# A two-layer graph network kernel: where sums, counts and normalizations are computed in layer 0

## Chip, cores and metric

One core of one Trainium2 chip. The metric is the device time of one execution in microseconds (us). The engines are TensorE (PE; its weight loads are shown as PEld), VectorE (DVE), ScalarE (ACT), GpSimd (POOL) and SyncE (SP), which issues most of the transfers.

## What is computed

A residual network of two message-passing layers over 6,250 nodes of 128 features and 206,250 edges, sorted by destination. Cut to what matters:

```python
h = relu(layernorm(x))
summed = segment_sum(h[src], dst); counts = segment_sum(ones, dst)
agg = summed / max(counts, 1)
x = x + log_softmax(agg @ W_l.T + h @ W_r.T + b)        # layer 0
h = relu(layernorm(x))
weight = relu(edge_attr @ W1 + b1) @ W2 + b2
x = x + segment_sum((h @ Wl + bl)[dst] * weight, src)   # layer 1
```

The layernorm subtracts the mean of a node's 128 features and divides by the square root of their variance plus 1e-5.

## The kernel before, in words

Nodes lie in 49 blocks of 128 rows (partitions are nodes of a block). For the normalizations seven blocks make a chunk, so there are seven chunks of 128 x 896 elements. Each engine has one program in order, and semaphores tie the programs together; nothing is scheduled at run time, so the order written in the source is the order of each queue.

**Normalization (both layers).** `norm_mean` (L643) on VectorE sums each row of a chunk (L644), scales the sums to means (L645) and subtracts the means from the chunk (L646). `squares` (L1313) on ScalarE squares the result (L1317). `norm_var` (L722) on VectorE sums the squares (L724) and scales them (L725). `deviations` (L1319) on ScalarE takes the square root (L1321). `norm_relu` (L727) on VectorE takes the reciprocal (L729) and scales the positive part (L730). A `link` is a wait of VectorE for its own last instruction. In layer 0, `h0_cut` (L738, VectorE), `h0_high` (L1326, ScalarE) and `h0_low` (L520, GpSimd) then split each value into a high part and a low part, which lie in `h0p`, per block 128 high columns, 128 low columns and two columns of ones. The loop at L741 interleaves these steps: in pass c it takes the mean of one chunk, finishes the chunk of two passes before and sums the squares of the chunk of one pass before. ScalarE's loop at L1329 does, per pass, `squares` of this chunk, `deviations` of the chunk before, `h0_high` of the chunk three passes back.

**Layer 0.** 37 steps of two blocks each, 74 blocks in all, walk over the edges. Per block VectorE makes eight pairs of one-hot tables (`one_hots`, L769), four pairs of buffers deep; PE multiplies them to counts of edges (`step_counts`, L1111), ScalarE copies the counts out (L1360) and, in 32 of the steps, compares node numbers with thresholds (L1352). PE multiplies the finished counts of the block before by `h0p` (`dense`, L1120, 258 columns wide), so that 256 columns hold high and low sums and the last two hold the number of edges per destination. After that, `block_sums` (L774) on VectorE, which stands behind the second pair of one-hots of the next block, waits for the last of the dense products, then adds high and low sums (L777), copies the count (L778), makes a one-hot matrix that places rows at their nodes (L779), and makes a second one scaled by the counts in bf16 (L781). `place` (L1124) on PE, behind the fourth counting step of the block, multiplies the sums by the first matrix in fp32 (L1127) and a matrix of ones by the second in bf16 (L1128). `add_block` (L786) on VectorE, behind the sixth pair of one-hots, adds the two results into the aggregate (L789).

**Between the layers** the loop at L924 (and those at L1388 on ScalarE and L1203 on PE) runs logits, exponentials, logarithms, the second normalization and the product with `Wl`, chunk by chunk, in one interleaved order. **Layer 1** (L1023, L1287, L1462 and the stream of messages, L605) takes the rest of the time.

## Time and profile before

| | |
|---|---|
| median of 3 runs | 3699.18 us (3697.62 to 3706.08) |
| the profiled execution, its own time | 3703.27 us |
| its span in the trace | 3701.4 us |
| PE, VectorE, ScalarE, GpSimd busy | 3077.9, 2796.2, 2089.7, 2207.1 us |
| mean granted TensorE clock, share of full | 0.93 |

The stretches of the span: preparation to about 80 us, the first normalization being its second half; layer 0 to about 910 us; the stage between the layers to 1037 us; layer 1 to the end. In a view of instructions, a number in brackets is the idle time of the engine just before, with the work that ended it. Instructions of one engine overlap at their ends in the trace, so what one of them costs its queue is the distance from its start to the next one's start.

### The profile page before, as it was taken

To read this page: it belongs to the slowest core of one execution; us is meant where nothing else is said; L and a number is where in the kernel's file an instruction comes from. 1 tells how busy PE (TensorE), PEld (TensorE's weight loads), DVE (VectorE), ACT (ScalarE), POOL (GpSimd) and SP (SyncE) were. 2 spreads that over 40 slices of the span, in tenths; PEclk is the share of its full clock that TensorE was granted. 3 is DMA by queue.
4 is the path that set the end of the run, shared out by engine and by line. 5 is a ranking of instruction groups with operands and counts; after the bars stand their busy time and mean duration, and the time that the engine had idled before them with its cause. 6 is when DMAs were issued, how large, how long until landed. Compare 5 with 4: busy or idle time off the path is not lost.

```text
span 3701.4 us, 97235 instructions
## 1 busy us (share of the span) xinstructions
PE 3077.9 (83%) x26330; PEld 2498.3 (67%) x26331; DVE 2796.2 (76%) x7718; ACT 2089.7 (56%) x4907; POOL 2207.1 (60%) x1790
## 2 busy tenths in 40 slices
PE   1799999998677779888888888898888888888867
PEld 0699999997555557666666666666667766666656
DVE  8899999998855557886676766767677777877756
ACT  2699999994532235554454544554455545545546
POOL 4300101000357777777878787878878777878860
PEclk9999999998777779998998989999899999999989
DMA  3298998801034446766776666665677667767757
GB/s 110 70 337 315 319 319 316 316 7 36 12 70 88 88 104 162 175 157 145 151 154 152 135 145 145 154 154 132 144 166 173 161 147 172 172 141 165 174 118 207
DMA packets 576963, 592.90 MB, mean 160 GB/s; under 512 B 71050, under 2 KB 557954, under 8 KB 576689
## 3 DMA queue, kind: packets, MB, share of 16 engines
q1 hardware_dynamic: 449506, 470.49, 44.1%
q0 software_dynamic: 127184, 119.07, 18.2%
q8 instruction: 134, 2.20, 0.2%
q14 instruction: 139, 1.14, 0.1%
HBM read 293.94 MB, written 295.35 MB: 159 GB/s over the span
## 4 chain that ended last, share of the span: by engine, by line
PE 27%; DVE 26%; issue 18%; DMA 12%; POOL 11%; DVEq 5%; ACT 2%; SPq 0%; POOLq 0%; ACTq 0%
DMA messages<-big,idxr 11%; POOL messages L605 10%; PE PS L1120 10%; DVE X L1018 5%; PE PS L1111 5%; PE PS L1283 4%; DVE big L991 3%; DVE aux L769 3%; PE PS L1250 2%; DVE hpar L1007 2%; DVEq L1013 2%; DVE big L965 2%; DVE big L979 2%; PE PS L1262 2%; DVE big L968 1%
## 5 line engine op out<-in xcount | busy, mean ns | idle before, releaser
L605 POOL DMA_INDIRECT messages<-big,idxr x1664 | 2035.5, 1223 | 552.5 <-issue 462.4
L1283 PE MATMUL PS<-big,hpar 128*128 128x128 f32 x5120 | 677.5, 287 | 215.3 <-DVE hpar L1007 163.3
L1283 PEld LDWEIGHTS PS<-big,hpar 128*128 128x128 f32 x5120 | 623.8, 199 | 275.6 <-DVE hpar L1007 217.6
L1433 ACT ACTIVATE big<-PS,b1c 128x512 f32<-128x512 f32 x416 | 285.8, 687 | 788.5 <-PE PS L1239 788.5
L1018 DVE TENSOR_TENSOR X<-X,PS 128x128 f32 x1280 | 367.9, 287 | 315.3 <-issue 93.0
L1120 PE MATMUL PS<-h_parts,counts 128*128 128x258 f32 x3626 | 565.3, 296 | 0.0
L1360 ACT ACTIVATE counts<-PS 128x784 fp32r<-128x784 f32 x592 | 481.3, 825 | 94.3 <-PE PS L1111 85.2
L1250 PE MATMUL PS<-W2s,big 128*128 128x128 f32 x3328 | 524.3, 305 | 0.0
L1250 PEld LDWEIGHTS PS<-W2s,big 128*128 128x128 f32 x3328 | 439.5, 206 | 101.6 <-issue 101.6
L1444 ACT ACTIVATE big<-PS 128x512 f32<-128x512 f32 x416 | 247.5, 595 | 405.7 <-PE PS L1262 402.4
L1120 PEld LDWEIGHTS PS<-h_parts,counts 128*128 128x128 f32 x3626 | 469.6, 191 | 0.2 <-ACT counts L1360 0.2
L509 POOL DMA_INDIRECT KLg<-edge_keys,tj_i x37 | 69.8, 1887 | 625.5 <-PE PS L1091 597.4
L1262 PE MATMUL PS<-hpar,big 128*128 x4992 | 411.2, 229 | 27.7 <-issue 17.3
L1456 ACT ACTIVATE big<-iotaF,big 128x128 f32<-128x128 f32 x1280 | 406.3, 395 | 39.6 <-DMA big<-messages 37.8
L991 DVE TENSOR_TENSOR big<-PS,big 128x512 f32<-128x512 f32 x416 | 284.2, 683 | 161.7 <-PE PS L1250 161.5
L769 DVE TENSOR_TENSOR aux<-iotaLq,cols 128x1024 bf16<-128x1024 bf16 x592 | 406.0, 686 | 0.4
L1262 PEld LDWEIGHTS PS<-hpar,big 128*128 128x128 bf16 x4992 | 357.4, 103 | 62.8 <-issue 37.3
L1111 PE MATMUL PS<-aux 128*128 128x98 bf16 x4736 | 316.3, 211 | 61.8 <-DVE aux L769 61.1
L769 DVE TENSOR_TENSOR aux<-iotaKq,cols 128x784 bf16<-128x784 bf16 x592 | 339.7, 574 | 0.0
L1239 PE MATMUL PS<-big,W1s 64*128 64x256 f32 x1664 | 324.0, 469 | 0.0
L1111 PEld LDWEIGHTS PS<-aux 128*128 128x128 bf16 x4736 | 242.9, 99 | 99.6 <-DVE aux L769 80.0
L1269 PE MATMUL PS<-big,onesb 128*128 128x250 bf16 x416 | 118.7, 285 | 173.2 <-DVE idxr L985 165.3
(222 smaller groups left out, 3823.3 us busy)
## 6 DMA issues: line engine op xcount, KB each, us to landing
messages<-zeros SPq DMA_DIRECT2D x896, 193.5 KB
big<-messages SPq DMA_DIRECT2D x320, 516.0 KB
aux<-slot_rows SPq DMA_DIRECT2D x416, 128.0 KB
big<-in_edge_attr_dram SPq DMA_DIRECT2D x402, 128.0 KB
messages<-big,idxr POOLq DMA_INDIRECT x1664
X<-in_x_dram SPq DMA_DIRECT2D x12, 448.0 KB, 6.8
out_dram<-X SPq DMA_DIRECT2D x6, 448.0 KB
edge_places<-big SPq DMA_DIRECT2D x1, 2496.0 KB, 13.2
```

The lines of the kernel that those rows point to most:

```text
L605: pool.indirect_dma_start(strm_d, bass.IndirectOffsetOnAxis(ap=idxr[:, n % U, j:j + 1], axis=0), outr[:, n % U, j, :], None, compute_op=AL ...
L769: last = nc.vector.tensor_tensor(oh[:, o % NOH, :, :, :], numbers.unsqueeze(1).to_broadcast([P, Q // few, width, few]), cols[:, n % 2, w, ...
L991: nc.vector.tensor_tensor(outr[:, k, :, 0:C], pW.rearrange("p (j c) -> p j c", j=J), hgs[:, k % 2, :].rearrange("p (j c) -> p j c", j=J), ...
L1018: nc.vector.tensor_tensor(Xf[:, ds(at, C)], Xf[:, ds(at, C)], sums[:, r * C:(r + 1) * C], ALU.add)\
L1111: last = nc.tensor.matmul(psB[:, o % 2, s, 0:KD], ohl[:, o % NOH, s // IL, :, s % IL], ohk[:, o % NOH, s // IK, :, s % IK], start=True, st ...
L1120: last = nc.tensor.matmul(psD[:, h, :], Bc[h][:, b, :], h0p[:, b, :], start=(b == 0), stop=(b == NB - 1))
L1239: last = nc.tensor.matmul(pHID[:, h, :].rearrange("p (q e) -> p q e", q=2), W1s[h * R:(h + 1) * R, :], attrT[h * R:(h + 1) * R, k % 2, :, ...
L1250: last = nc.tensor.matmul(pW[:, j * C:(j + 1) * C], hidT[:, k % 2, j * P:(j + 1) * P], W2s[:, :], start=False, stop=(j == J - 1))
L1262: last = nc.tensor.matmul(pHG[:, j * C:(j + 1) * C], oht[:, k % 2, j * P:(j + 1) * P], h1p[:, ds(at + a * C, C)], start=(a == 0), stop=(a ...
L1283: last = nc.tensor.matmul(to[:, r * C:(r + 1) * C], finhot[:, n % 2, r * 2 + q, :], fin[:, k, r, q * ROW:q * ROW + C], start=(q == 0), sto ...
L1360: nc.scalar.activation(Bc[h][:, :, o * Q * D:(o + 1) * Q * D].rearrange("p b (s d) -> p b s d", s=Q), psB[:, o % 2, :, 0:KD].rearrange("p ...
L1456: last = nc.scalar.activation(away[:, t, :], iotaF[:, :], ACT.Abs, bias=fin[:, k, r, q * ROW + C:(q + 1) * ROW])
```

## The change

VectorE's sum of high and low parts now spans 129 columns instead of 128, because `h0p` is laid out as 128 high columns, a column of ones, 128 low columns and a column of zeros: the last of the 129 is the count. The copy of the count, the matrix scaled by it and the wait between them go. `place` computes the counts' product in fp32, with the column of counts, repeated 128 times, as the stationary operand and the first one-hot matrix as the moving one. In both normalizations VectorE's subtraction and the scaling of the variance go; ScalarE subtracts the mean with seven activations per chunk (one for each block, the mean being a bias per partition) and takes the scale of the variance into its square root. GpSimd fills the two columns with two instructions instead of one.

```diff
...
-        aggv = sb("aggv", [P, 2, C], fp32)
+        aggv = sb("aggv", [P, 2, C + 1], fp32)
         ohv = sb("ohv", [P, 2, 2, P], fp32)
-        cntv = sb("cntv", [P, 2], fp32)
-        ohc = ohv[:, :, 1, :].bitcast(bf16)[:, :, 0:P]
...
-            x_zero tables_ready h0_ready sq_done std_ready wT_done wT_ready strm_zero
+            x_zero tables_ready h0_ready mean_ready sq_done std_ready wT_done wT_ready strm_zero
...
             def h0_low(n):
                 c = NCH - 1 - n
                 pool.wait_ge(S["h0_cut"], n + 1)
-                nc.gpsimd.tensor_tensor(h0p[:, chunk(c), C:2 * C], H[:, chunk(c), :], resid[:, n % 2, :].rearrange("p (b c) -> p b c", c=C),
+                nc.gpsimd.tensor_tensor(h0p[:, chunk(c), C + 1:2 * C + 1], H[:, chunk(c), :], resid[:, n % 2, :].rearrange("p (b c) -> p b c", c=C),
                                         ALU.subtract).then_inc(S["h0_low"], 1)
 
             def h0_back(c):
-                nc.gpsimd.tensor_tensor(H[:, chunk(c), :], h0p[:, chunk(c), 0:C].bitcast(fp32), h0p[:, chunk(c), C:2 * C].bitcast(fp32), ALU.add).then_inc(S["h0_back"], 1)
+                nc.gpsimd.tensor_tensor(H[:, chunk(c), :], h0p[:, chunk(c), 0:C].bitcast(fp32), h0p[:, chunk(c), C + 1:2 * C + 1].bitcast(fp32), ALU.add).then_inc(S["h0_back"], 1)
 
             biased = [0]
 
...
             for n in range(NCH):
                 h0_low(n)
             pool.wait_ge(S["h0_low"], NCH)
-            nc.gpsimd.memset(h0p[:, :, 2 * C:HW].bitcast(fp32), 1.0).then_inc(S["h0p_ready"], 1)
+            nc.gpsimd.memset(h0p[:, :, C:C + 1].bitcast(fp32), 1.0).then_inc(S["h0p_ready"], 1)
+            nc.gpsimd.memset(h0p[:, :, HW - 1:HW].bitcast(fp32), 0.0).then_inc(S["h0p_ready"], 1)
             bias_parts()
             for c in range(2, 4):
                 step_rows(c)
...
             def norm_mean(c):
                 link(nc.vector.tensor_reduce(mean[:, chunk(c)], X[:, chunk(c), :], AX, ALU.add))
-                link(nc.vector.tensor_scalar(mean[:, chunk(c)], mean[:, chunk(c)], 1.0 / C, None, ALU.mult))
-                nc.vector.tensor_tensor(H[:, chunk(c), :], X[:, chunk(c), :], bc(mean[:, chunk(c)]), ALU.subtract)\
-                    .then_inc(S["lnT"], 1)
+                nc.vector.tensor_scalar(mean[:, chunk(c)], mean[:, chunk(c)], -1.0 / C, None, ALU.mult).then_inc(S["mean_ready"], 1)
 
             dve.wait_ge(S["consts"], NCONST)
             nc.vector.tensor_scalar(ident[:, :], iotaF[:, :], iotaP[:, 0:1], None, ALU.is_equal).then_inc(S["d_consts"], 1)
...
             def norm_var(c, n, slot):
                 dve.wait_ge(S["sq_done"], n + 1)
-                link(nc.vector.tensor_reduce(var[:, chunk(c)], E1[:, slot, :].rearrange("p (b c) -> p b c", c=C), AX, ALU.add))
-                nc.vector.tensor_scalar(var[:, chunk(c)], var[:, chunk(c)], 1.0 / C, None, ALU.mult).then_inc(S["lnT_copied"], 1)
+                nc.vector.tensor_reduce(var[:, chunk(c)], E1[:, slot, :].rearrange("p (b c) -> p b c", c=C), AX, ALU.add)\
+                    .then_inc(S["lnT_copied"], 1)
 
             def norm_relu(c, n, ready):
                 dve.wait_ge(S["std_ready"], n + 1)
...
             def block_sums(q, c2, h):
                 dve.wait_ge(S["dense_done"], q + 1)
                 wait(dve, S["sums_done"], q - 1)
-                nc.vector.tensor_reduce(aggv[:, h, :], psD[:, h, 0:2 * C].rearrange("p (a c) -> p c a", a=2), AX, ALU.add)
-                nc.vector.tensor_copy(cntv[:, h:h + 1], psD[:, h, 2 * C:2 * C + 1]).then_inc(S["aggv_ready"], 1)
-                nc.vector.tensor_scalar(ohv[:, h, 0, :], iotaF[:, :], nid[:, ds(c2, 1), h], None, ALU.is_equal)
-                dve.wait_ge(S["aggv_ready"], q * 2 + 1)
-                nc.vector.tensor_scalar(ohc[:, h, :], iotaF[:, :], nid[:, ds(c2, 1), h], cntv[:, h:h + 1], ALU.is_equal, op1=ALU.mult)\
-                    .then_inc(S["aggv_ready"], 1)
+                nc.vector.tensor_reduce(aggv[:, h, :], psD[:, h, :].rearrange("p (a c) -> p c a", a=2), AX, ALU.add)
+                nc.vector.tensor_scalar(ohv[:, h, 0, :], iotaF[:, :], nid[:, ds(c2, 1), h], None, ALU.is_equal).then_inc(S["aggv_ready"], 1)
 
             base_regs = [dve.alloc_register(f"base{h}") for h in range(2)]
 
...
             def dense(q, h, o):
                 if o == 1:
                     pe.wait_ge(S["counts_out"], (q + 1) * OPB)
-                    wait(pe, S["aggv_ready"], (q - 1) * 2)
+                    wait(pe, S["aggv_ready"], q - 1)
                 for b in range(BPO * (o - 1), min(NB, BPO * o)):
                     last = nc.tensor.matmul(psD[:, h, :], Bc[h][:, b, :], h0p[:, b, :], start=(b == 0), stop=(b == NB - 1))
                 if o == OPB - 1:
                     last.then_inc(S["dense_done"], 1)
 
             def place(q, h):
-                pe.wait_ge(S["aggv_ready"], q * 2 + 2)
+                pe.wait_ge(S["aggv_ready"], q + 1)
                 wait(pe, S["agg_done"], q)
-                nc.tensor.matmul(psR[:, 0, :], aggv[:, h, :], ohv[:, h, 0, :], start=True, stop=True)
-                nc.tensor.matmul(psR[:, 1, :], onesb[:, :], ohc[:, h, :], start=True, stop=True).then_inc(S["sums_done"], 1)
+                nc.tensor.matmul(psR[:, 0, :], aggv[:, h, 0:C], ohv[:, h, 0, :], start=True, stop=True)
+                nc.tensor.matmul(psR[:, 1, :], aggv[:, h, C:C + 1].to_broadcast([P, P]), ohv[:, h, 0, :], start=True, stop=True)\
+                    .then_inc(S["sums_done"], 1)
 
             step_columns(0, 0)
 
...
                 for h in range(2):
                     for o in range(OPB):
                         if known and c == 0 and h == 1 and o == 1:
-                            pe.wait_ge(S["h0p_ready"], 1)
+                            pe.wait_ge(S["h0p_ready"], 2)
                             pe.wait_ge(S["h0_high"], NCH)
                             pe.wait_ge(S["h0_low"], NCH)
                             pe.wait_ge(S["wT_ready"], 1)
...
         @block.scalar
         def _(act):
             def squares(c, n, slot, lag):
+                act.wait_ge(S["mean_ready"], n + 1)
+                for b in range(c * CB, (c + 1) * CB):
+                    last = nc.scalar.activation(H[:, b, :], X[:, b, :], ACT.Identity, bias=mean[:, b:b + 1])
+                last.then_inc(S["lnT"], 1)
                 act.wait_ge(S["lnT"], n + 1)
-
                 wait(act, S["lnT_copied"], n - lag)
                 nc.scalar.activation(E1[:, slot, :], H[:, chunk(c), :].rearrange("p b c -> p (b c)"), ACT.Square).then_inc(S["sq_done"], 1)
 
             def deviations(c, n):
                 act.wait_ge(S["lnT_copied"], n + 1)
-                nc.scalar.activation(var[:, chunk(c)], var[:, chunk(c)], ACT.Sqrt, bias=epsc[:, :]).then_inc(S["std_ready"], 1)
+                nc.scalar.activation(var[:, chunk(c)], var[:, chunk(c)], ACT.Sqrt, bias=epsc[:, :], scale=1.0 / C).then_inc(S["std_ready"], 1)
 
             def h0_high(n):
```

## Rows read from the trace of the kernel before

**Rows 1.** The profile's page, busy time of each engine.
```profile
PE 3077.9 (83%) x26330; PEld 2498.3 (67%) x26331; DVE 2796.2 (76%) x7718; ACT 2089.7 (56%) x4907; POOL 2207.1 (60%) x1790
```

**Rows 2.** Busy time by stretches: window, its length, engines, PE clock, DMA share, GB/s.
```profile
35.00:80.50 45.50, 1.38 (x4) 0.58 (x4) 44.61 (x57) 16.02 (x22) 19.08 (x11) 1.00 0.05 14
...
113.00:177.00 64.00, 48.14 (x494) 43.31 (x494) 61.75 (x141) 31.81 (x47) 21.29 (x16) 0.94 0.19 55
177.00:880.00 703.00, 670.20 (x7857) 640.29 (x7857) 676.76 (x1445) 649.21 (x1466) 63.54 (x31) 1.00 0.74 258
...
944.40:988.60 44.20, 25.76 (x150) 21.30 (x149) 42.22 (x51) 30.15 (x34) 17.32 (x8) 0.80 0.00 0
944.40:1004.00 59.60, 36.54 (x193) 29.66 (x193) 54.28 (x65) 40.69 (x47) 25.61 (x12) 0.75 0.07 18
...
1037.00:3701.40 2664.40, 2231.39 (x17184) 1707.75 (x17184) 1848.64 (x5770) 1296.81 (x3264) 2035.51 (x1664) 0.92 0.65 148
```

**Rows 3.** Timeline of VectorE in one block of layer 0: start, duration, engine, line.
```profile
408.66 0.42 DVE L777 TENSOR_REDUCE aggv<-PS 128x128 f32<-128x256 f32 x1 [0.24 <-PE PS L1120]
409.00 0.15 DVE L778 COPY cntv<-PS 128x1 f32<-128x1 f32 x1
409.06 0.28 DVE L779 TENSOR_SCALAR ohv<-iotaF,nid 128x128 f32<-128x128 f32 x1
409.26 0.34 DVE L781 TENSOR_SCALAR ohv<-iotaF,nid,cntv 128x128 bf16<-128x128 f32 x1
409.51 0.68 DVE L769 TENSOR_TENSOR aux<-iotaLq,cols 128x1024 bf16<-128x1024 bf16 x1
```

**Rows 4.** Timeline of PE in the same block.
```profile
402.91 0.38 PE L1127 MATMUL PS<-ohv,aggv 128*128 128x128 f32 x2
403.13 0.22 PE L1128 MATMUL PS<-ohv,onesb 128*128 128x128 bf16 x1
403.19 0.54 PE L1111 MATMUL PS<-aux 128*128 128x98 bf16 x8
...
410.73 0.55 PE L1111 MATMUL PS<-aux 128*128 128x98 bf16 x8 [0.53 <-DVE aux L769]
```

**Rows 5.** Groups by line, 177 to 880 us: count, busy, mean ns, idle before, releaser.
```profile
L1360 ACT ACTIVATE counts<-PS 128x784 fp32r<-128x784 f32 x537 | 435.9, 824 | 53.9 <-PE PS L1111 44.8 <-issue 3.0
...
L1111 PE MATMUL PS<-aux 128*128 128x98 bf16 x4304 | 282.3, 209 | 32.8 <-DVE aux L769 32.8
...
L777 DVE TENSOR_REDUCE aggv<-PS 128x128 f32<-128x256 f32 x68 | 28.8, 424 | 19.7 <-PE PS L1120 19.7
L789 DVE TENSOR_TENSOR big<-big,PS 128x256 f32 x67 | 28.2, 422 | 6.5 <-PE PS L1128 6.5
```

**Rows 6.** Timeline of VectorE in one pass of the first normalization.
```profile
54.74 1.08 DVE L644 TENSOR_REDUCE mean<-X 128x7 f32<-128x896 f32 x1
55.85 1.15 DVE L645 TENSOR_SCALAR mean<-mean 128x7 f32<-128x7 f32 x1
57.04 1.09 DVE L646 TENSOR_TENSOR hpar<-X,mean 128x896 f32<-128x896 f32 x1
58.05 0.19 DVE L729 RECIPROCAL var<-var 128x7 f32<-128x7 f32 x1
...
59.28 1.08 DVE L724 TENSOR_REDUCE var<-aux 128x7 f32<-128x896 f32 x1
...
60.51 0.63 DVE L738 TENSOR_SCALAR big<-hpar 128x896 int32<-128x896 int32 x1
```

**Rows 7.** Timeline of ScalarE: the first normalization, then four activations of layer 1.
```profile
38.27 1.28 ACT L1321 ACT_TABLE_LOAD   x1
39.57 0.30 ACT L1321 ACTIVATE var<-var,epsc 128x7 f32<-128x7 f32 x1
40.84 0.95 ACT L1317 ACTIVATE aux<-hpar 128x896 f32<-128x896 f32 x1 [0.97 <-DVE hpar L646]
...
2002.75 1.27 ACT L1456 ACTIVATE big<-iotaF,big 128x128 f32<-128x128 f32 x4
```

## Prediction

> **What bounds the kernel now.** I read the page first. PE, VectorE and GpSimd are all busy most of the time [rows 1], and such averages decide nothing, so I went on to the busy time by stretches [rows 2]. The change touches three of them. In the first normalization (35 to 80.5 us) VectorE is busy 44.61 of 45.50 us and ScalarE only 16.02: VectorE is the bound. In layer 0 (177 to 880 us) PE has 670, VectorE 677 and ScalarE 649 of 703 us: three engines nearly full, so the waits between them must be read. Between the layers (944.4 to 988.6 us) VectorE has 42.22 of 44.20 us, ScalarE 30.15. The last 2,664 us are layer 1, which the change does not touch.
>
> What to see in layer 0: 68 blocks lie in that window, 703 / 68 = 10.34 us each. VectorE waits 19.7 us (0.29 a block) for the last dense product before its sum L777, and PE waits 32.8 us (0.48 a block) for the next one-hots [rows 5]. These are one hand-over, seen from both sides: dense products end, VectorE does L777 to L781 and then a pair of one-hots, and PE, with only two pairs in hand, stands for 0.53 us [rows 4] before the third. From there to the end of the block PE runs through. So each block is a chain of VectorE's few instructions and then PE's products, and what either of them loses or gains shows in full.
>
> **Layer 0, VectorE's side.** From start to start, L778 costs 409.06 - 409.00 = 0.06 us and L781 409.51 - 409.26 = 0.25 us [rows 3]. Both go: 0.31 us a block. The sum reads 258 elements where it read 256; at 0.34 us for 256 that is 0.003 us, nothing. The removed wait cost nothing of its own, since the copy had ended (409.15) before L781 began.
>
> **Layer 0, PE's side.** The first product of `place`, fp32, is two records and takes 403.13 - 402.91 = 0.22 us of PE's order; the second, bf16, 403.19 - 403.13 = 0.06 us [rows 4]. In fp32 on the same shape I take 0.22, so +0.16 us a block, and PE has nothing to hide it behind. No row shows a weight load from one repeated column. Bounds: nothing added, if it overlapped wholly, and +0.70 us, if its two records and their loads lay end to end twice as long as the pair's 0.38 us (0.76 in place of 0.06). I take the near row, 0.16. The result for L789 comes 0.16 us later; behind that add only one-hots and the wait before L777 are queued, and its 0.29 us of idle time takes the delay in. ScalarE, 53.9 us idle before its copies [rows 5], loses part of that when PE comes earlier and stays under PE.
>
> Net 0.31 - 0.16 = 0.15 us a block, 68 x 0.15 = 10.2 us. The four blocks of 113 to 177 us, where VectorE has 61.75 of 64.00 us and PE 48.14 [rows 2], are VectorE's alone: 4 x 0.31 = 1.2. The last two blocks I leave at nothing. Sum for layer 0: **-11.4 us**; bounds -22.3 (72 x 0.31, PE's price hidden) and +25.3 (68 x 0.39 - 1.2).
>
> **First normalization.** VectorE sheds the subtraction, 58.05 - 57.04 = 1.01 us, and a link, some 0.1 us: a linked sum holds its queue 55.85 - 54.74 = 1.11 us, an unlinked instruction of that length 1.01 [rows 6]. The stretch from the sum of squares to the cut, 60.51 - 59.28 = 1.23 us, becomes 1.01. Six of the seven subtractions lie here (the first is taken while the edge lists still load), so 6 x 1.11 + 7 x 0.22 = 8.2 us.
>
> ScalarE takes seven activations of 128 x 128 per chunk. The nearest row, four of that shape with a bias per partition, takes 1.27 us [rows 7], so seven take 7 x 0.32 = 2.2 us. A later pass of ScalarE is then 2.2 + 0.95 (Square) + 0.30 (Sqrt) + 0.95 (h0_high, the size of Square) = 4.4 us. VectorE's pass shrinks from 5.77 us plus the cut of about 0.5 to some 5.0 us, so ScalarE stays hidden, with 0.6 us to spare. Not so in the first pass, where the square root also needs its table, 1.28 us [rows 7], and stands behind the seven activations: 2.2 + 0.95 + 1.28 + 0.30 = 4.7 us after the mean, while VectorE comes to the reciprocal after L724 and the next mean, 1.01 + 1.11 + 0.1 = 2.2 us. A new wait of 2.5 to 2.6 us. I take 8.2 - 2.6 = **-5.5 us** (rounded); bounds 0 and -8.2. Layer 0 starts that much earlier, because its start and the clearing of the aggregate follow this stage in order. GpSimd's second fill is one more short instruction ahead of the bias preparation, which nobody waits for at that point; without that cover it would cost its own length, some 0.1 to 0.2 us.
>
> **Between the layers.** Per chunk VectorE sheds 1.33 us and ScalarE gains 2.2. From 944.4 to 988.6 us VectorE falls from 42.2 to 42.2 - 5 x 1.33 = 35.6 us, ScalarE rises from 30.15 to 30.15 + 4 x 2.2 = 39.0: the bound moves to ScalarE. With the 2.0 us of waits that VectorE had as the bound, that is 41.0 of 44.2: -3.2 us. In the following 15.4 us ScalarE's 40.69 - 30.15 = 10.5 becomes 14.9, with the waits 16.9: +1.5 us. **-1.7 us**; bounds -9.3 (7 x 1.33) and +7.6 (7 x (2.2 - 1.11)).
>
> **Sum.** -11.4 - 5.5 - 1.7 = -18.6 us. The profiled execution took 3703.27 us (span 3701.4), 4.1 above the median of 3699.18; its differences carry over, so 3684.7 for such an execution and **3680.6 us** for the median.
>
> **Rivals.** About 0.2%, 7.4 us, is what a measurement of this kernel can tell from no change: below 3691.8 is faster, above 3706.6 slower.
>
> First, the normalizations give nothing, because ScalarE becomes their bound in both. For it: 2.2 us replace 1.01 us of VectorE. Against it: ScalarE's 16 of 45.5 us in the first one. 3699.2 - 11.4 = 3687.8 us; 0.15. The Trainium skill (ScalarE: Activation LUTs, section Rules for kernel authors) speaks against the change here: it says to give additions and multiplications to VectorE rather than ScalarE. The trace agrees on the price, and by the rule alone this rival's 3687.8 would be the result.
>
> Second, layer 0 gives nothing, because with three engines at 92 to 96% another of them, ScalarE above all, takes up the hand-over. Against it: the waits of rows 5. 3699.2 - 5.5 - 1.7 = 3692.0 us; 0.13.
>
> Third, slower: the counts' product with its repeated column runs serially. It decides once that product takes more than 0.06 + 0.31 + (1.2 + 5.5 + 1.7) / 68 = 0.49 us in PE's order; at its bound of 0.76 the time is 3699.2 + 25.3 - 7.2 = 3717.3 us. Against it: the fp32 neighbour's 0.22. 0.06.
>
> Fourth, the new function makes ScalarE load a table for every chunk and another for the square root: in the first normalization its pass is 4.4 + 2.6 = 7.0 against 6.3 us (6 x 0.7 = +4), between the layers 7 x 1.28 - 1.7 = +7.3, in all -0.1, 3699.1 us. Against it: Square follows Sqrt without a load [rows 7]. 0.04. The skill's page (same title, section Table sets) counts this function among those in every set; no row here shows it.
>
> Fifth, PE hides its price: 3699.2 - 22.3 - 7.2 = 3669.7 us; 0.04.
>
> **Numbers.** The forecast has 0.58. The range runs from the fifth case to just past the second, 3669 to 3694; outside lie the third, the fourth and the forecast's own misses, under 0.2 together. Faster: 0.56 of the forecast, 0.14 of the first, 0.06 of the second (it sits on the border), 0.04 of the fifth, 0.80. Slower: the third and 0.01, 0.07. The rest, 0.13, is the same.
>
> **What would show it.** Right: in layer 0, 10.2 us a block, PE's idle time before the third counting step near 0.17 us, four records of 0.11 us in `place`, VectorE's sum to one-hots 0.54 us; in the first normalization seven activations about 0.3 us apart, one wait of 2.6 us before the first reciprocal, layer 0 some 5.5 us earlier; between the layers ScalarE nearly full. Wrong: PE's wait unchanged, a record above 0.2 us from start to start in the counts' product, or table loads ahead of the seven activations.

## The result, and the profile after

The changed kernel takes 3670.78 us (median of 4 runs, 3668.92 to 3679.85) against 3700.24 for the kernel before on the same chip: a ratio of 0.9923, 95% interval 0.9902 to 0.9944. The forecast was 3680.6 us, with a range of 3669 to 3694. The profiled execution is the slowest of the four: 3679.85 us, span 3678.0. Two executions among the experiments were disturbed, the profiled one of the last kernel (4279.81 us at a granted clock of 0.626, so no stage is read from it) and one of another kernel (9235.73 us); times and ratios below leave both out.

The total hides more than it shows, so I cut the span at three events that every kernel has: the first one-hots of layer 0, its last block sum, and the first transpose of layer 1. The stages are those of one profiled execution of each kernel.

```
kernel (profiled execution)   to first one-hots   layer 0   between   layer 1   span
before                                     81.1     825.8     130.0    2664.5   3701.4
after                                      75.7     813.4     123.4    2665.5   3678.0
after less before                          -5.4     -12.4      -6.6      +1.0    -23.4
```

The page of the kernel after, busy time of each engine (to be held against [rows 1]): VectorE has 176 instructions and 41.4 us less, ScalarE 31.3 us more.

```profile
PE 3090.6 (84%) x26404; PEld 2506.4 (68%) x26405; DVE 2754.8 (75%) x7542; ACT 2121.0 (58%) x5005; POOL 2205.0 (60%) x1791
```

Busy time by stretches of the kernel after, columns as in [rows 2]: the first normalization, 68 blocks of layer 0, the second normalization from the first chunk's mean to the last's, layer 1.

```profile
35.00:75.00 40.00, 1.38 (x4) 0.58 (x4) 36.50 (x45) 27.84 (x64) 18.69 (x11) 1.00 0.06 18
...
170.00:865.00 695.00, 683.08 (x7934) 652.65 (x7933) 657.78 (x1314) 652.00 (x1468) 63.48 (x31) 1.00 0.76 261
925.05:980.79 55.74, 34.24 (x192) 27.71 (x190) 49.02 (x53) 53.36 (x89) 23.99 (x12) 0.79 0.07 20
1012.50:3678.00 2665.50, 2239.46 (x17184) 1709.38 (x17184) 1847.00 (x5770) 1297.92 (x3264) 2037.48 (x1664) 0.92 0.67 148
```

In layer 0 the same 68 blocks need 695 us, 10.22 each, where they needed 703; PE is now at 98%. Between the layers ScalarE is nearly full (53.36 of 55.74 us) and VectorE no longer.

VectorE in one block of layer 0 after, to be held against [rows 3]:

```profile
409.06 0.43 DVE L774 TENSOR_REDUCE aggv<-PS 128x129 f32<-128x258 f32 x1 [0.26 <-PE PS L1113]
409.40 0.28 DVE L775 TENSOR_SCALAR ohv<-iotaF,nid 128x128 f32<-128x128 f32 x1
409.60 0.69 DVE L766 TENSOR_TENSOR aux<-iotaLq,cols 128x1024 bf16<-128x1024 bf16 x1
```

From the sum to the next one-hots it is 0.54 us; it was 0.85. PE in the same kernel, to be held against [rows 4]:

```profile
403.24 0.38 PE L1120 MATMUL PS<-ohv,aggv 128*128 128x128 f32 x2
403.46 0.39 PE L1121 MATMUL PS<-ohv,aggv 128*128 128x128 f32 x2
403.68 0.54 PE L1104 MATMUL PS<-aux 128*128 128x98 bf16 x8
```

The counts' product holds PE's order for 403.68 - 403.46 = 0.22 us, 0.16 more than its bf16 forerunner. The groups of 170 to 865 us, to be held against [rows 5]:

```profile
L1357 ACT ACTIVATE counts<-PS 128x784 fp32r<-128x784 f32 x539 | 438.0, 826 | 43.4 <-PE PS L1104 29.7 <-issue 2.7
...
L1104 PE MATMUL PS<-aux 128*128 128x98 bf16 x4305 | 282.6, 209 | 11.9 <-DVE aux L766 7.6
...
L774 DVE TENSOR_REDUCE aggv<-PS 128x129 f32<-128x258 f32 x68 | 29.1, 428 | 17.0 <-PE PS L1113 17.0
L782 DVE TENSOR_TENSOR big<-big,PS 128x256 f32 x67 | 28.2, 421 | 20.3 <-PE PS L1121 17.8
```

PE's wait for one-hots falls from 32.8 to 11.9 us, 0.48 to 0.175 us a block. The add L782 waits 0.30 us a block instead of 0.10, and the wait ahead of the sum shrinks from 0.29 to 0.25: part of the delay of the counts was taken in there.

The first normalization, timeline of ScalarE and VectorE after (to be held against [rows 7]): seven activations 0.31 us apart, the square's pass, the table, and VectorE's long wait at the first reciprocal (a second one is 0.7 us).

```profile
36.38 2.15 ACT L1310 ACTIVATE hpar<-X,mean 128x128 f32<-128x128 f32 x7 [21.94 <-DVE mean L644]
38.57 0.95 ACT L1314 ACTIVATE aux<-hpar 128x896 f32<-128x896 f32 x1
39.54 1.28 ACT L1318 ACT_TABLE_LOAD   x1
40.83 0.30 ACT L1318 ACTIVATE var<-var,epsc 128x7 f32<-128x7 f32 x1
...
41.16 0.20 DVE L726 RECIPROCAL var<-var 128x7 f32<-128x7 f32 x1 [2.42 <-ACT var L1318]
```

### The profile page after: what moved, and what is told of

It reads as the page before. It is cut to its first block, busy times and chain, and to the rows that moved or that the text cites. A ratio compares the mean times of both kernels' runs of the same rounds, so it can differ in the third digit from the quotient of the medians.

```text
span 3678.0 us, 97210 instructions
## 1 busy us (share of the span) xinstructions
PE 3090.6 (84%) x26404; PEld 2506.4 (68%) x26405; DVE 2754.8 (75%) x7542; ACT 2121.0 (58%) x5005; POOL 2205.0 (60%) x1791
## 4 chain that ended last, share of the span: by engine, by line
DVE 26%; PE 25%; issue 19%; DMA 11%; POOL 11%; DVEq 5%; ACT 2%; SPq 0%; POOLq 0%; ACTq 0%
DMA messages<-big,idxr 11%; POOL messages L604 10%; PE PS L1113 10%; DVE X L1011 6%; PE PS L1104 5%; DVE big L984 3%; PE PS L1277 3%; DVE aux L766 3%; PE PS L1244 2%; DVE hpar L1000 2%; DVEq L1006 2%; DVE big L972 2%; DVE big L958 2%; DVE big L969 1%; DVE big L961 1%
## 5 line engine op out<-in xcount | busy, mean ns | idle before, releaser
L1277 PE MATMUL PS<-big,hpar 128*128 128x128 f32 x5120 | 667.3, 284 | 188.9 <-DVE hpar L1000 145.0
L1277 PEld LDWEIGHTS PS<-big,hpar 128*128 128x128 f32 x5120 | 616.1, 197 | 246.4 <-DVE hpar L1000 195.6
L1244 PE MATMUL PS<-W2s,big 128*128 128x128 f32 x3328 | 531.9, 308 | 0.0
L1104 PE MATMUL PS<-aux 128*128 128x98 bf16 x4736 | 316.4, 211 | 38.4 <-DVE aux L766 32.9
L1104 PEld LDWEIGHTS PS<-aux 128*128 128x128 bf16 x4736 | 246.0, 99 | 76.1 <-DVE aux L766 55.9
```

The lines of the kernel that those rows point to most:

```text
L1104: last = nc.tensor.matmul(psB[:, o % 2, s, 0:KD], ohl[:, o % NOH, s // IL, :, s % IL], ohk[:, o % NOH, s // IK, :, s % IK], start=True, st ...
L1244: last = nc.tensor.matmul(pW[:, j * C:(j + 1) * C], hidT[:, k % 2, j * P:(j + 1) * P], W2s[:, :], start=False, stop=(j == J - 1))
L1277: last = nc.tensor.matmul(to[:, r * C:(r + 1) * C], finhot[:, n % 2, r * 2 + q, :], fin[:, k, r, q * ROW:q * ROW + C], start=(q == 0), sto ...
```

## The experiments

### First set: one part at a time

**Blocks only:** sums and counts as after, both normalizations as before.

```diff
-                nc.vector.tensor_scalar(mean[:, chunk(c)], mean[:, chunk(c)], -1.0 / C, None, ALU.mult).then_inc(S["mean_ready"], 1)
+                link(nc.vector.tensor_scalar(mean[:, chunk(c)], mean[:, chunk(c)], 1.0 / C, None, ALU.mult))
+                nc.vector.tensor_tensor(H[:, chunk(c), :], X[:, chunk(c), :], bc(mean[:, chunk(c)]), ALU.subtract)\
+                    .then_inc(S["lnT"], 1)
...
-                for b in range(c * CB, (c + 1) * CB):
-                    last = nc.scalar.activation(H[:, b, :], X[:, b, :], ACT.Identity, bias=mean[:, b:b + 1])
...
```

> The new block of layer 0 with the normalizations as before. Theory (three separate terms, read from the two traces): the first one-hots of layer 0 start at 80.5 us as before, layer 0 and its tail take 12.5 us less (last block's sum 906.9 - 12.5 = 894.4), and the stage between the layers gains nothing that the normalization gave: at most the 2 us by which PE's products ran at a higher granted clock there. Whole span 12 to 15 us less than before. Rival (the terms hang together: the hand-over in layer 0 only shrinks because VectorE arrives otherwise after the new normalization): layer 0 gains under 6 us.

Measured: 3700.91 us, ratio 1.0002 (0.9992 to 1.0012). Layer 0 took 813.1 us, 12.7 less than before, as the theory had it, and yet the total stood still.

**Norms only:** the normalizations as after, sums and counts as before.

```diff
-                nc.vector.tensor_reduce(aggv[:, h, :], psD[:, h, :].rearrange("p (a c) -> p c a", a=2), AX, ALU.add)
+                nc.vector.tensor_reduce(aggv[:, h, :], psD[:, h, 0:2 * C].rearrange("p (a c) -> p c a", a=2), AX, ALU.add)
+                nc.vector.tensor_copy(cntv[:, h:h + 1], psD[:, h, 2 * C:2 * C + 1]).then_inc(S["aggv_ready"], 1)
...
-                nc.tensor.matmul(psR[:, 1, :], aggv[:, h, C:C + 1].to_broadcast([P, P]), ohv[:, h, 0, :], start=True, stop=True)\
-                    .then_inc(S["sums_done"], 1)
+                nc.tensor.matmul(psR[:, 1, :], onesb[:, :], ohc[:, h, :], start=True, stop=True).then_inc(S["sums_done"], 1)
...
```

> Both normalizations new, the block of layer 0 as before. Theory: first one-hots 5.4 us earlier (75.1 us), layer 0 unchanged to 1 us plus 1 to 2 us in its tail, the stage between the layers 4.5 to 6.5 us less; whole span 10 to 14 us less. Rival (ScalarE bounds the stage between the layers, as the prediction reckoned): that stage only 1.7 us less, whole span 7 us less.

Measured: 3708.14 us, ratio 1.0019 (1.0006 to 1.0032), slower than the kernel before. Its stages say otherwise: first one-hots at 76.5 us (-4.6), between the layers 125.3 us (-4.7); layer 0 took 826.3 us, and the 1 to 2 us expected of its tail did not come.

That tail, from the last sum but one to the last, takes 17.2 us in before and 15.6 in after. In it GpSimd adds high and low parts back together, four chunks in a row, and four small instructions of VectorE that run meanwhile, 0.2 to 0.3 us each otherwise, take 8.1 us together in before and 6.9 in after. GpSimd's four chunks and one of these instructions, in before and then in after:

```profile
896.08 8.55 POOL L524 TENSOR_TENSOR hpar<-h_parts 128x896 f32<-128x896 f32 x4
896.11 2.11 DVE L834 SCALAR_TENSOR_TENSOR halves<-halves,extra 128x48 f32<-128x48 f32 x1
```

```profile
879.74 7.32 POOL L522 TENSOR_TENSOR hpar<-h_parts 128x896 f32<-128x896 f32 x4
881.61 1.81 DVE L827 SCALAR_TENSOR_TENSOR halves<-halves,extra 128x48 f32<-128x48 f32 x1
```

Norms only, which keeps the old layout of `h0p`, has before's 2.08 us a chunk, and every trace with the new layout, blocks only among them, has 1.77. So some 1.2 us of the tail's 1.5 come with the layout.

**Second normalization back** on VectorE, all else as after (`norm_mean(i - 3, True)` takes the old path, and ScalarE's activations run for the first normalization alone):

```diff
-                    norm_mean(i - 3)
+                    norm_mean(i - 3, True)
...
```

> The changed kernel with the second normalization on VectorE again. Theory: the stage between the layers loses what the normalization gave there, 4 to 5 us of its 6.5, so layer 1 starts about 1016.5 to 1017 us instead of 1012.5; everything up to the last block of layer 0 as in the changed kernel. Rival (ScalarE is the bound of that stage and the gain came from PE's clock): layer 1 starts at 1012.5 us or earlier.

Measured: 3698.05 us, ratio 0.9996 (0.9984 to 1.0008), 27 us slower than after (on another chip), from one normalization. But between the layers it took 123.2 us, no more than after's 123.4. By the numbers that is the rival's outcome (layer 1 begins at 1010.6 us); the section Between the layers shows that the move's gain is in there all the same.

**Counts' product twice:**

```diff
+                nc.tensor.matmul(psR[:, 1, :], aggv[:, h, C:C + 1].to_broadcast([P, P]), ohv[:, h, 0, :], start=True, stop=True)
```

> The counts' product is computed twice per block. Theory (PE has no cover for it): each block takes 0.22 us more, 68 blocks 15 us; last block's sum at 889.1 + 15 = 904. Rival (part of PE's price is hidden behind the wait for the one-hots, 0.175 us a block idle): 0 to 4 us more.

Measured: 3695.83 us in a single run; layer 0 took 828.6 us, 15.2 more than after, 15.2 / 68 = 0.22 us a block. What PE is given in `place` shows in full, at the price read from the timeline: there is no cover for it.

The first normalization and layer 0 thus change as forecast, and the totals don't. What differs is layer 1, whose code none of these kernels touches: 2664.5, 2665.5 and 2664.1 us in before, after and counts twice, but 2677.4, 2678.5 and 2682.9 us in the other three.

### Where layer 1 loses 13 to 25 us

Busy time by stretches put the loss in one place, 3030 to 3260 us. That is layer 1's sixth loop: its steps are written as seven loops (`LOOPS`, L44), and the sixth has 5 rounds. The waits of VectorE in that loop, blocks only:

```profile
DVE big L960 <- issue: 20.2, 4, 5.4
```

Four waits of some 5 us with no releaser, one at each turn of the loop, at its first line. One of them in the timeline:

```profile
3077.80 0.72 ACT L1455 ACTIVATE hpar<-big,onesf 128x512 f32<-128x512 f32 x1
...
3079.41 0.37 DVE L960 TENSOR_TENSOR big<-iotaB,blcol 128x200 bf16<-128x200 bf16 x1 [5.09 <-issue]
...
3081.32 2.07 PE L1279 MATMUL PS<-big,hpar 128*128 128x128 f32 x8 [5.36 <-DVE hpar L1002]
```

VectorE stands for 5.09 us, and then PE for 5.36 us behind it. In the kernel after the same line shows this in the same loop (3060 to 3262 us):

```profile
DVE big L958 <- issue: 1.4, 4, 0.4
```

A round of that loop is 304 instructions of VectorE in every kernel, but the change shortens VectorE's program ahead of it, each variant by another number. Hence the theory: VectorE loads its code in blocks, and where a round lies across one block more, each turn has to load code again. Four kernels test it. They add instructions at the start of VectorE's program, where it waits 8.2 us for its constants; two such waits make one instruction.

```diff
+            for _ in range(56):
+                dve.wait_ge(S["consts"], 1)
             dve.wait_ge(S["consts"], NCONST)
```

**After, 28 instructions more** (the edit above):

> The kernel after, with 28 more instructions at the start of VectorE's program (waits on a semaphore that is already set, while VectorE idles for its constants anyway). Theory of place: layer 1 is slower by 13 to 18 us where the 304 instructions of a round of its sixth loop (5 rounds) lie so in VectorE's program that each turn of the loop has to load code again; 28 instructions put that loop where the blocks-only kernel has it. So four waits of VectorE of 4.6 to 5.7 us without a releaser at the first line of a step, some 54 us apart, between 3050 and 3260 us; about 161 to 164 packets in the second instruction queue; layer 1 2677 to 2683 us; total 3684 to 3692 us. Rival (layer 1's length is a matter of the run, or of the data that the normalizations leave): no such waits, layer 1 2655 to 2666 us, total 3669 to 3674 us.

Measured: 3691.43 us, ratio 0.9979 (0.9970 to 0.9988). Layer 1 took 2687.6 us in the profiled execution, the longest of the eleven, 4.6 more than the theory's end. VectorE's waits from 3060 to 3262 us:

```profile
DVE big L960 <- issue: 20.9, 4, 5.5
```

**After, 60 more** (`range(120)`):

> The kernel after, with 60 more instructions at the same spot: every loop of layer 1 then begins at the same instruction of VectorE's program as in the kernel before. Theory of place: the waits of VectorE of 2.9 to 3.3 us at the turns of the first loop and of 5.4 us at the seventh's turn, which after has and before hasn't, are gone; about 139 packets in the second instruction queue; layer 1 2655 to 2665 us, total 3660 to 3672 us, and the difference to the kernel before is that of layer 0 and of the stretch between the layers alone (-5.4, -11 to -12, -6.5 at most). Rival (the turns of first and seventh loop cost nothing because GpSimd's rows are late anyway): total within 2 us of after, 3669 to 3673 us. If the 60 instructions take over 8 us at the start, the first one-hots come later by the rest.

Measured: 3676.5 us, ratio 0.9940 (0.9927 to 0.9953), layer 1 2662.5 us. The same line, in the same loop (3050 to 3252 us):

```profile
DVE big L960 <- issue: 1.3, 4, 0.3
```

The 60 instructions cost nothing that shows at the start (first one-hots at 76.1 us). The total lies above what either side expected, and on another chip than after; the intervals of the two overlap, so whether the turns of first and seventh loop cost anything in sum is not settled. Layer 1 is only 3 us shorter than after's.

**Blocks only, 32 more** (`range(64)`):

> The blocks-only kernel (new sums and counts, old normalizations), with 32 more instructions at the start of VectorE's program: the loops of layer 1 lie as in the kernel before. Theory of place: the four waits of about 5 us in the sixth loop are gone, layer 1 is 2664 to 2666 us as in the kernel before, and the 12.7 us that layer 0 gave come out at the end: 3686 to 3690 us. Rival (something in layer 1 takes back what layer 0 gives, a slower clock or GpSimd's rows): 3699 to 3702 us as without the shift.

Measured: 3683.74 us, ratio 0.9961 (0.9947 to 0.9975), layer 1 2663.4 us: without the shift the same kernel had 1.0002. Layer 0's 12.8 us now come out at the end (3698.34 for before on this chip, less 3683.74, is 14.6, some 2 us more than expected).

**Second normalization back, 46 more** (`range(92)`):

> The kernel after with the second normalization's subtraction and scaling back on VectorE, and with 46 more instructions at the start of VectorE's program: loops of layer 1 as in the kernel before, so it stands beside the kernel after with 60. Theory that the second normalization's move gives what was forecast: 1.7 us slower than that one (and 6.5 us slower if the whole gain between the layers in the profile of after was the move's). Rival (the gain between the layers is of TensorE's clock and the tail, not of the move): within 1 us of it. Theory of place: 16 to 22 us faster than the same kernel without the shift, 3676 to 3682 us.

Measured: 3683.51 us, ratio 0.9955 (0.9943 to 0.9968), layer 1 2666.8 us; without the shift 0.9996, so the shift gives some 15 us, just under what the theory of place had. It is 7.0 us slower than after with 60 more, where 1.7 were expected and the rival had 1, though the intervals of the two ratios overlap; the section Between the layers takes this apart.

All kernels together; "begins" is the number of VectorE's instructions ahead of the sixth loop, in the program as built, and what is left of it modulo 128; packets are those of the instruction queue q14 on the page.

```
kernel                        begins  mod 128   waits at its turns   q14   layer 1
before                          4298       74          none          139    2664.5
after                           4238       14          none          152    2665.5
counts twice                    4238       14          none          152    2664.1
blocks only                     4266       42     4 of about 5 us    163    2677.4
norms only                      4270       46     4 of about 5 us    164    2678.5
second norm. back               4252       28     4 of about 5 us    162    2682.9
after, 28 more                  4266       42     4 of about 5 us    164    2687.6
after, 60 more                  4298       74          none          140    2662.5
blocks only, 32 more            4298       74          none          140    2663.4
second norm. back, 46 more      4298       74          none          139    2666.8
```

The theory of place holds in every row: one program with and without a shift loses and regains the waits, with nothing else in it changed. Packets of q14 hold 8.2 KB (1.14 MB / 139). After with 28 more has 24 packets more than with 60 more, for five turns that load (four here, one in the seventh loop). The seventh loop, also 304 instructions, waits 4.5 to 5.6 us at its turn where it begins at 30, 44, 58 or 62, not at 90; the first, of 328, waits 2.9 to 3.3 us at each turn where it begins at 58, not at 72, 86, 90 or 118; the second, of 304, begins at 16, 84, 98, 112 or 116 and never waits. Blocks of 128 instructions and room for three, with the program's start 56 to 64 instructions into a block, give all of these; that is an inference from the traces, not something that they show. The Trainium skill (Runtime: NRT & Kernel Launch, section Instruction fetch mechanics) says that a taken branch to code which is no longer at hand stalls until it is loaded; the traces are in keeping with that, at 4.6 to 5.7 us a turn in this loop, but show no load as such. The blocks of 256 instructions and the window of two that the Trainium skill gives in the same section would fit the loops of 304 too, but not the first loop's waits in after and counts twice, where 826 instructions of VectorE's program stand ahead of it.

### Second set: the chain of a block, and a faster version

These have the loops of layer 1 where before has them, and stand beside after with 60 more (layer 0 813.0 us).

**One-hot first:**

```diff
-                dve.wait_ge(S["dense_done"], q + 1)
...
-                nc.vector.tensor_reduce(aggv[:, h, :], psD[:, h, :].rearrange("p (a c) -> p c a", a=2), AX, ALU.add)
-                nc.vector.tensor_scalar(ohv[:, h, 0, :], iotaF[:, :], nid[:, ds(c2, 1), h], None, ALU.is_equal).then_inc(S["aggv_ready"], 1)
+                nc.vector.tensor_scalar(ohv[:, h, 0, :], iotaF[:, :], nid[:, ds(c2, 1), h], None, ALU.is_equal)
+                dve.wait_ge(S["dense_done"], q + 1)
+                nc.vector.tensor_reduce(aggv[:, h, :], psD[:, h, :].rearrange("p (a c) -> p c a", a=2), AX, ALU.add).then_inc(S["aggv_ready"], 1)
```

> The kernel after with the one-hot of a block's number (L775) put ahead of the wait for the dense products instead of behind the sum, and with the loops of layer 1 where the kernel before has them (as in the kernel after with 60 more instructions, 3676.5 us, layer 0 813.0 us). Theory that VectorE's way from the dense sum to the next one-hots (0.54 us: 0.34 the sum, 0.20 the one-hot) is the chain of a block: it shortens to 0.34 us, layer 0 loses up to 0.17 to 0.20 us a block, 68 times, 11.5 to 13.5 us: 800 to 802 us, total 3663 to 3666 us. Rival (ScalarE, which is busy 652 of the 695 us of that stretch, or the placing products which then start later, set the block): layer 0 not below 809 us, total 3672 to 3677 us.

Measured: 3666.47 us, ratio 0.9903 (0.9888 to 0.9918); layer 0 797.3 us, 15.7 less, 2.2 more than the theory's end; where these 2.2 come from was not tried. Groups and a stretch of this kernel, 170 to 850 us:

```profile
L1106 PE MATMUL PS<-aux 128*128 128x98 bf16 x4312 | 282.7, 209 | 1.2 <-DVE aux L768 1.0
L777 DVE TENSOR_REDUCE aggv<-PS 128x129 f32<-128x258 f32 x68 | 29.0, 427 | 2.3 <-PE PS L1115 0.2
```

```profile
170.00:850.00 680.00, 678.85 (x7945) 653.26 (x7944) 656.76 (x1315) 643.22 (x1468) 31.26 (x31) 1.00 0.77 267
```

The hand-over is gone from both sides: PE waits 1.2 us in all for one-hots, VectorE 2.3 ahead of the sum, and PE is busy 678.85 of 680 us. In this kernel PE is the bound of layer 0.

**Counts as bf16:** upper halves of the same fp32 values.

```diff
-                nc.tensor.matmul(psR[:, 1, :], aggv[:, h, C:C + 1].to_broadcast([P, P]), ohv[:, h, 0, :], start=True, stop=True)\
+                nc.tensor.matmul(psR[:, 1, :], aggv[:, h, C:C + 1].bitcast(bf16)[:, 1:2].to_broadcast([P, P]),
+                                 ohv[:, h, 0, :].bitcast(bf16).rearrange("p (n w) -> p n w", w=2)[:, :, 1], start=True, stop=True)\
```

> The kernel after with the product that places the counts made of the upper halves of the same fp32 counts and one-hots, read as bf16, and with the loops of layer 1 as in the kernel before. Theory that the 0.16 us that the fp32 product takes longer on TensorE than the four bf16 counting rows of before lie on the chain of a block (as twice the product gave 0.22 us for each of 68 blocks): layer 0 loses 0.12 to 0.16 us a block, 8 to 11 us: 802 to 805 us, total 3665 to 3669 us. Rival (once shorter, TensorE waits for the next one-hots instead, 0.17 us of idle time before a block's third counting step): layer 0 811 to 813 us, total 3674 to 3677 us.

Measured: 3669.77 us, ratio 0.9909 (0.9894 to 0.9924); layer 0 800.9 us, 12.1 less. PE in a block:

```profile
409.29 0.22 PE L1123 MATMUL PS<-ohv,aggv 128*128 128x128 bf16 x1
409.35 0.53 PE L1106 MATMUL PS<-aux 128*128 128x98 bf16 x8
```

The product holds PE for 0.06 us instead of 0.22, and that 0.16, 10.9 us over 68 blocks, comes out whole.

**Early table:**

```diff
...
+            act.wait_ge(S["consts"], NCONST)
+            nc.scalar.activation(thr_s[:, :], epsc[:, :], ACT.Sqrt)
```

> The kernel after with one more Sqrt of a single column at the start of ScalarE's program, so that its table is there before the first normalization, and with the loops of layer 1 as in the kernel before. Theory: of the 2.4 us for which VectorE waits at L726 the table load is about 1.3 us, so that wait becomes 1.0 to 1.3 us and the first one-hots come 1.1 to 1.4 us earlier; total 3674 to 3676 us, which five rounds cannot tell from none. Rival (the seven activations ahead of the squares alone set the wait, or the table is loaded again): wait 2.2 to 2.6 us, first one-hots within 0.3 us of the kernel without it.

Measured: 3680.86 us, ratio 0.9942 (0.9928 to 0.9955), no difference that can be told. The wait at the first reciprocal is halved, to the theory's 1.2 us. The first one-hots come at 74.7 us, 1.4 earlier than in after with 60 more; but over all kernels with these normalizations they come between 74.7 and 77.0, so that alone shows nothing. VectorE's waits from 35 to 75 us:

```profile
DVE var L729 <- ACT var L1321: 1.8, 2, 1.2
```

**Together**, the three edits, 28 instructions of shift, and

```diff
-    LOOPS = ((3, 4), (5, 2), (4, 4), (4, 4), (3, 4), (5, 2), (2, 2))
+    LOOPS = ((3, 4), (5, 2), (4, 4), (4, 4), (6, 2), (5, 2), (2, 2))
```

> The three edits together (one-hot ahead of the wait, counts as bf16, early table), layer 1's fifth loop as 6 rounds of 2 instead of 3 rounds of 4 (304 instructions of VectorE a round instead of 604), and 28 instructions at the start of VectorE's program, so that of layer 1's loops only the third and fourth (535 instructions) load code at their turns. Theories: a block of layer 0 takes 9.9 us instead of 10.2 if the terms add (layer 0 790 us), or 10.05 if ScalarE sets it once both are shorter (800 us); the two waits of about 5 us at the turns of the fifth loop go: layer 1 2652 to 2660 us instead of 2662 to 2667; or, as for first and seventh loop, GpSimd's rows hide them: 2662 to 2667 us. Total 3640 to 3650 us by the first of each, 3660 to 3667 us by the second of each.

Measured: 3652.11 us, ratio 0.9851 (0.9832 to 0.9871), 51.5 us below the kernel before on that chip and faster than every other version. It is nearer to the sum of the first of each theory than to the second. No stage is read from its trace, but the turns of the loops can be. VectorE's waits at the first line of a step, in after with 60 more from 2730 to 2850 us (two turns of the fifth loop as it was) and in this kernel from 3200 to 3450 us (five turns of the new one):

```profile
DVE big L960 <- issue: 10.3, 2, 5.5
```

```profile
DVE big L961 <- issue: 1.7, 5, 0.4
```

The waits are gone, and of all seven loops only the third and the fourth still have them (2.9 to 3.6 us), as was expected. How much that gave in the total, and whether the two terms of layer 0 add, stays open.

### Between the layers

The stage took 130.0 us in before, 123.4 in after and in after with 28 more, 116.3 in after with 60 more. I cut it at the first and last chunk's mean (L643). In before the chunks take 1003.52 - 944.36 = 59.16 us; in second normalization back 59.11 and, with the shift, 59.18 us; in after 55.74 and in after with 60 more 55.03 us. So the move gives 3.4 to 4.1 us here. What follows the last mean goes mostly by PE's clock. Stretch from first to last mean and the rest, after with 60 more:

```profile
925.05:980.08 55.03, 33.27 (x196) 27.33 (x194) 48.33 (x53) 53.21 (x88) 23.70 (x12) 0.81 0.07 20
980.08:1005.40 25.32, 14.61 (x86) 11.32 (x86) 18.32 (x21) 16.51 (x26) 0.00 (x0) 0.87 0.00 0
```

The same rest in after, and in before:

```profile
980.80:1012.50 31.70, 21.57 (x87) 16.34 (x86) 18.38 (x21) 16.36 (x26) 0.00 (x0) 0.61 0.00 0
```

```profile
1003.50:1036.90 33.40, 23.21 (x94) 17.89 (x92) 19.73 (x24) 14.17 (x18) 0.00 (x0) 0.60 0.00 1
```

And both in second normalization back, unshifted:

```profile
924.87:983.98 59.11, 37.38 (x192) 30.18 (x191) 53.79 (x65) 40.68 (x47) 25.57 (x12) 0.75 0.07 19
983.98:1010.60 26.62, 15.96 (x92) 12.38 (x91) 19.67 (x24) 14.17 (x18) 0.00 (x0) 0.82 0.00 0
```

At a mean granted clock of 0.82 to 0.87 the rest is 25 to 27 us long, at 0.61 it is 32. By windows of 10 us from 979.1 on, after has 0.67, 0.50, 0.51 and after with 60 more 0.67, 0.99, 0.87; the two levels are 1.2 and 2.4 GHz. The clock is not all of it: before and after have nearly the same clock in the rest, and after is 1.7 us shorter. Over all traces with a clock of 0.50 to 0.61 there, the rest takes 32.9 to 33.5 us with the second normalization on VectorE (three kernels) and 31.5 to 32.2 with it moved (seven), so some 1.4 us of the move lie there, as far as kernels at nearly the same clock can tell. Ahead of the first mean the length goes with the clock: 37.2 to 37.9 us at 0.68 to 0.70, 35.6 to 36.0 at 0.76 to 0.81, with either normalization. The unshifted kernel with the second normalization back thus lost 3.4 us on the chunks and 1.5 ahead of the first mean (37.4 us against 36.0), and won 5 in the rest, so that its stage came out equal; that explains its miss. Shifted, its profiled execution had a rest of 32.0 us at 0.66 beside 25.3 at 0.87 in after with 60 more, so how much of the 7.0 us between the medians of these two is the move's can't be told. What decides which level the stretch gets was not tried.

## Why the prediction was right, and where it was not

- **Layer 0, VectorE's side:** right. 0.85 to 0.54 us from sum to one-hots, the 0.31 forecast.
- **Layer 0, PE's side:** right, and shown by two runs: 0.16 us, no cover. Twice the product cost 0.22 us a block, and the bf16 form gave the 0.16 back. The rival of a serial product and that of a hidden price both fall.
- **Sum for layer 0:** -11.4 forecast, -12.4 to -12.8 in the traces. The step "The last two blocks I leave at nothing" is the mis-sized term: from the first one-hots to the last sum but one, after is 10.9 us shorter than before, and the tail from there to the last sum another 1.5 us. Of the tail, 1.2 us come with the layout of `h0p` (norms only, above), to which the prediction gave no time.
- **First normalization:** right. One wait of 2.42 us (2.6 forecast), first one-hots 5.4 us earlier in after (5.5 forecast; 4.1 to 6.4 over all kernels with this normalization); the early table took 1.2 us of that wait away, so the load was in it as priced. No load stands ahead of a chunk's activations, ScalarE loads 20 tables in after as in before, and the fourth rival falls.
- **Between the layers:** "-1.7 us" was too small. The bound did move to ScalarE, but of -3.2 and +1.5 only the first came: the chunks take 3.4 us less. Of the other 3.2 us of the profile's -6.6, 1.7 lie behind the last mean at nearly the same clock, for which the sum has no term, and 1.5 ahead of the first mean are PE's clock, which no step had and which can go either way.
- **"The last 2,664 us are layer 1, which the change does not touch":** here the working was wrong in kind, and the result right by luck. The change moves every loop of layer 1 in VectorE's program by 60 instructions. They came to lie where the sixth loop turns freely; shifted by 28 instructions the same work takes 15 us longer than shifted by 60 (3691.43 against 3676.5 us), and of the gain 6.9 us are left (3698.34 - 3691.43). A rival for this was missing.
- **The sum:** -18.6 forecast, -29.5 measured (3670.78 - 3700.24), near the lower end of the range. With the loops where before has them the runs give 3676.5 - 3698.34 = -21.8 us, and the traces' terms -5.4 - 12.6 - 3.4 - 1.4 = -22.8. The rest of after's own -29.5 lies in four runs that spread over 11 us, and isn't explained by any experiment. Both rivals in which a part gives nothing fall with the stages of blocks only and norms only. The Trainium skill (ScalarE: Activation LUTs, section Rules for kernel authors) wants additions kept on VectorE; the trace agrees on the price (2.15 us of ScalarE for seven blocks, for 1.01 of VectorE) and not on the outcome here, where VectorE was the bound.

## What to carry to other kernels

Where two engines wait for each other once a block, read the few instructions between the two waits: each tenth of a microsecond there counts once a block, and what could be done ahead of the wait (the one-hot) cost nothing there. Compare kernels by the duration of each stage before believing a total, and look into a stage whose code is the same in both. A loop of a few hundred instructions can change its time by the number of instructions ahead of it; long waits at the first line of each round, most of them without a releaser, are the sign, and a few idle instructions at the program's start, where its engine waits anyway, are test and cure.

## What was not expected of the hardware

- A turn of a VectorE loop of 304 instructions costs 0.3 us or 4.6 to 5.7 us, by place alone; in the kernels with four such turns layer 1 was 13 to 25 us longer.
- Loops with more instructions a round (535 and 604) show waits of 2.9 to 5.9 us at each of their eight turns in every trace of a kernel with these loops; the view puts some of them down to a product of PE, and four to eight to nothing.
- The stretch behind the second normalization's last mean takes 25 or 32 us by the granted clock (0.87 or 0.61) with the same program in it.
- A 128x128x128 fp32 product whose stationary operand is one column, repeated, costs PE's order 0.22 us, as its fp32 neighbour does, and with the upper halves read as bf16 0.06 us.
- GpSimd's sum of two parts of 128 x 896 elements takes 2.08 us where the second begins 128 columns behind the first and 1.77 us where it begins 129 behind.
